# Cross-attention block with a four-layer FFN: both first transposes of the probabilities moved behind the third step of the second FFN layer

## The reference

```python
x = x + xattn(layernorm(x), ctx)     # 8 heads of 32, causal mask, softmax over 77 keys
x = x + ffn(layernorm(x))
# ffn: h = silu(x w1 * s1) * (x w2 * s2)       256 -> 1024
#      h = gelu(h h1 * s)                      1024 -> 1024
#      h = gelu(h h2 * s)                      1024 -> 1024
#      out = h w3 * s3                         1024 -> 256
```

## Time and profile before

| | us |
|---|---|
| median of 3 runs | 1674.82 (1674.29 to 1677.77) |
| the profiled execution, its own time | 1673.74 |
| its span in the profile | 1671.6 |
| PE busy | 1617.4 (97%) |
| PE weight loads | 1311.9 (78%) |
| DVE busy | 806.5 (48%) |
| ACT busy | 783.5 (47%) |
| POOL busy | 139.4 (8%) |

### The profile page before, as it was taken

One profiled execution on the slowest core, in us unless ns is written; L12 is line 12 of the kernel. 1 busy time (PEld: TensorE's weight loads), 2 busy tenths in 40 slices (PEclk: granted clock), 3 DMA queues, 4 the chain that ended last, 5 costly groups with the idle time before them and its releaser, 6 DMA issues.

```text
span 1671.6 us, 22062 instructions
## 1 busy us (share of the span) xinstructions
PE 1617.4 (97%) x9006; PEld 1311.9 (78%) x9006; DVE 806.5 (48%) x1255; ACT 783.5 (47%) x1126; POOL 139.4 (8%) x136
## 2 busy tenths in 40 slices
PE   5599999999999999999999999999999999999998
PEld 4378788787887878878787887878878787887887
DVE  5563634637255463634637255463544636345331
ACT  4463644636345363543636345363543635345342
POOL 1101102010010200102010010200102010010000
PEclk7699999999999999999999999999999999999999
DMA  8100000010000100000010000100001010000000
GB/s 328 43 1 26 29 25 29 0 42 13 25 29 0 54 0 25 29 25 29 0 42 13 25 29 0 52 2 25 29 11 43 0 40 14 25 30 1 1 13 13
DMA packets 17638, 48.40 MB, mean 29 GB/s; under 512 B 5584, under 2 KB 7760, under 8 KB 16208
## 3 DMA queue, kind: packets, MB, share of 16 engines
q1 hardware_dynamic: 17616, 48.09, 8.0%
HBM read 39.63 MB, written 8.45 MB: 29 GB/s over the span
## 4 chain that ended last, share of the span: by engine, by line
PE 88%; DVE 6%; ACT 3%; issue 2%; DMA 0%; POOL 0%; POOLq 0%; SPq 0%; ACTq 0%
PE ffn_banks L348 69%; PE att_banks L484 4%; PE att_banks L503 3%; PE att_banks L456 3%; PE att_banks L472 2%; PE att_banks L493 2%; PE att_banks L447 2%; DVE probs L702 1%; DVE total L698 1%; ACT L579 1%; ACT probs L579 1%; DVE a_f L662 1%; PE att_banks L442 1%; PE att_banks L511 1%; DVE a_lo L667 1%
## 5 line engine op out<-in xcount | busy, mean ns | idle before, releaser
L348 PE MATMUL ffn_banks<-a_hi,h_sb 128*128 128x512 f32 x1024 | 408.9, 399 | 0.0
L348 PE MATMUL ffn_banks<-b_hi,h_sb 128*128 128x512 f32 x1024 | 401.3, 392 | 0.0
L348 PE MATMUL ffn_banks<-a_lo,h_sb 128*128 128x512 f32 x1024 | 400.2, 391 | 0.0
L348 PE MATMUL ffn_banks<-b_lo,h_sb 128*128 128x512 f32 x1024 | 398.6, 389 | 0.0
L554 ACT ACTIVATE a_f<-ffn_banks,vec 128x512 f32<-128x512 f32 x128 | 88.2, 689 | 354.2 <-PE ffn_banks L348 354.2
L673 DVE TENSOR_TENSOR a_lo<-a_f,a_hi 128x512 fp32r<-128x512 f32 x128 | 88.6, 692 | 317.8 <-ACT a_hi L555 317.8
L348 PEld LDWEIGHTS ffn_banks<-a_hi,h_sb 128*128 128x128 f32 x1024 | 192.3, 188 | 48.9 <-issue 6.2
L348 PEld LDWEIGHTS ffn_banks<-b_lo,h_sb 128*128 128x128 f32 x1024 | 192.3, 188 | 39.8
L348 PEld LDWEIGHTS ffn_banks<-b_hi,h_sb 128*128 128x128 f32 x1024 | 192.3, 188 | 39.8
L348 PEld LDWEIGHTS ffn_banks<-a_lo,h_sb 128*128 128x128 f32 x1024 | 192.5, 188 | 38.5
L348 PE MATMUL ffn_banks<-ln_hi,w_sb 128*128 128x512 f32 x512 | 213.8, 418 | 6.2 <-issue 6.2
(11 more groups left out here) (89 smaller groups left out, 1952.5 us busy)
## 6 DMA issues: line engine op xcount, KB each, us to landing
x_in<-in_x SPq DMA_DIRECT2D x16, 512.0 KB, 3.5
h_bits<-in_h SPq DMA_DIRECT2D x8, 1024.0 KB, 20.8
out<-out_sb SPq DMA_DIRECT2D x16, 512.0 KB, 2.6
ln_t<-in_x_t SPq DMA_DIRECT2D x15, 512.0 KB, 4.3
ln_rows<-ln_rows_dram SPq DMA_DIRECT2D x15, 512.0 KB, 3.8
w_bits<-in_w SPq DMA_DIRECT2D x3, 1024.0 KB, 10.1
ctx_sb<-in_ctx_t SPq DMA_DIRECT2D x16, 154.0 KB, 3.6
w_att_sb<-in_w_att SPq DMA_DIRECT2D x1, 512.0 KB, 5.8
```

The lines of the kernel that those rows point to most:

```text
L348: mm = nc.tensor.matmul(psum, left, right, start=(k == 0 and part == 0), stop=(k == rows - 1 and part == 1))
```

## The change

The list ORDER is changed in one line. The two first transposes stand together behind ("L2", 2), and ("SOFT", 1) stands behind both of them. FIRST is unchanged.

```diff
-    ("PT", 0), ("SOFT", 1), ("L2", 2), ("PT", 1), ("L2", 3), ("PV", 0), ("PT", 2), ("L2", 4), ("PT", 3),
+    ("L2", 2), ("PT", 0), ("PT", 1), ("SOFT", 1), ("L2", 3), ("PV", 0), ("PT", 2), ("L2", 4), ("PT", 3),
```

## The result

The changed kernel took 1730.64 us (median of 4 runs, 1727.26 to 1731.76) beside 1674.55 for the kernel before: a ratio of 1.0329 with a 95% interval of 1.0308 to 1.0350. Run again beside other kernels on another occasion it took 1731.69 us. The time lies in the forecast range, 1.2 us under the lower end of the rival in which the clock falls as well (1731.8 to 1740.8), and not near the likeliest case (1706.3).

A forecast was written before the change was run, and what follows sets the result against it. PE's order and waits bound the kernel, PT0 coming as late as half 0's scaling. PT2 2.10 us later in 15 passes (31.5 us), on 1673.74 plus 1.08 to the median, gave 1706.3 us; range 1702 to 1742.

The forecast's parts named there:

- the rival in which the clock falls as well: PE's clock also falls to half around PT2, in many or all woven passes: 1731.8 to 1740.8 us in all 15; chance 0.39.
- the likeliest case: Only waits move: PT2 2.10 us later in each of 15 passes, giving 1706.3 us, or 1703 to 1713 with spread.
- the order of the steps that the prediction lists: Chain before PT2: exponentials, Gelu table load, L2.2's two Gelus, DVE's subtraction, two copies, SOFT1; PT2 at 622.56 against 620.46.
- the lower bound: DVE's distance from one PSUM copy to the next instruction without a wait: at least 0.60 us, at most 0.78.
- PE's 1.05 us: Gain per pass for PE alone: 0.87 us of standing still before PT0 and one break of the stream less.
- the point from which the rival decides: At PT2, rival that SOFT1 is in time (1659.0 us, chance 0.04): SOFT1 must end by 620.34 to be no slower.
- the case with the clock up: Waits moved in the woven passes, PE's clock staying up or fallen in a few passes only; chance 0.53.
- the two slow cases: In the woven passes, waits moved with the clock up, 0.53, or the clock falling in many or all, 0.39.
- a stretch of 1.7 us: On PE from 609.35 to 611.07, with one group of transposes, it cost nothing; cited against the clock falling.
- The price of a fall: Time PE loses when its clock drops to half: at least 1.7 us, 2.3 for a longer fall.
- the later wait: PE standing still 2.2 us before PT2 for SOFT1, said to cover PV0's lateness of about 1.0 us.

The follow-up runs named there:

- e5: Changed kernel with 8 idle products on PE behind PV0, before PT2, in each of the 15 woven passes; 1704.87 us, ratio 1.0187 to the kernel before.
- e4: Changed kernel with PE's order kept, but ACT and DVE doing their part of L2.2 behind SOFT1; 1660.86 us, ratio 0.9910 to the kernel before.
- e6: Changed kernel with half 1's exponentials replaced by Gelu in the woven passes, so no table load before L2.2's Gelus; 1700.61 us, ratio 1.0158.
- e8: Changed kernel with 4 idle products on PE in the gap before PT2; 1707.87 us, ratio 1.0189 to the kernel before.
- e7: Changed kernel unaltered, run again beside other kernels; 1731.69 us, ratio 1.0342 to the kernel before.
- e2: Changed kernel with PT0 alone moved back in front of L2.2; 1707.03 us, ratio 1.0183 to the kernel before.
- e3: Changed kernel with SOFT1 alone moved back ahead of L2.2 and the two copies; 1688.83 us, ratio 1.0072 to the kernel before.
- e1: Changed kernel with 18 idle products on PE behind PV0, before PT2, in each of the 15 woven passes; 1735.49 us, ratio 1.0358.

## Why the prediction came out as it did

**Right: the direction and the mechanism.** PT2 now waits for SOFT1, SOFT1 for L2.2's subtraction and the copies, in the order of the steps that the prediction lists. Its terms, held against the changed kernel's second woven pass: from the table load's start to the scaling's end 221.75 + 1.45 - 215.60 = 7.60 us, forecast 622.44 - 614.81 = 7.63. The distance between the two copies, the only one the trace of before did not show, is 0.60 (in the third pass two copies begin at 321.49 and the sum behind them at 322.69), the lower bound. From the scaling's end to PT2 it is 223.25 - 223.20 = 0.05, forecast 0.12. PT2 is 1.98 us late, forecast 2.10, and these two small terms make up most of the difference; the waits cost 29.8 us (e5), forecast 31.5. PE's idling before PV0 and PT2 was forecast at 1.0 and 2.2 and is 0.94 and 1.95.

**Right: the gain that is lost.** e4 shows that PE's 1.05 us were there to be had, 1.00 as measured, and that the point from which the rival decides is where the prediction put it: SOFT1 has to be done before PE wants PT2.

**Right: the table load.** 1.28 us as in the earlier trace rows; e6 takes 1.31 off the period. The 1.38 us of drain besides it, which "ScalarE: Activation LUTs" of the Trainium skill states under "What ACT_TABLE_LOAD costs", are nowhere on this path: the Gelu starts 1.30 us behind the load's start (215.60 to 216.90).

**Wrong: which case is the likeliest.** The step that failed is the weighing of "The clock falls as well". I gave it 0.39 and the case with the clock up 0.53; it fell in 13 and 15 of 15 passes. (The chances of the two slow cases add up to 0.92, where the text has 0.93 for slower.) The first pass's fall after a stretch of 4.90 us with 2.26 us of work was the right row. I set against it that PV0 and PT2 are larger products than those of that stretch, and that a stretch of 1.7 us had cost nothing. Neither saved this kernel: the clock fell behind 5.0 us with 2.12 us of work, in two idle pieces of which none is longer than 2 us, and e5 and e8 show that it was this idling that took the clock, for with 0.9 and 1.8 us of it there is no fall.

The price of a fall was a little too high: I gave 1.7 us as the least, and the single falls cost 1.3 to 1.6, in part because several begin while PE still waits for PT2 (for the PT2 at 430.18 the clock is at half from 429.6 on). That the rival's lower end, 1731.8 for 1.7 us in each pass, agrees with the measured 1730.64 is partly luck: falls of double length in two passes (three in e7) bring the mean to 1.71 over fewer falls.

The Trainium skill's page "TensorE: Matmul & The Clock Gate" ("HAM oscillation — how this bites in real kernels") warns of gaps in which PE idles. Read as speaking of one wholly idle piece, it would have spared this kernel, whose longest piece is 1.95 us; the trace disagrees, with falls in 13 and 15 of 15 passes.

**Not foreseen:** what PT0's move does, which I had booked as harmless beside the later wait. It adds the idle piece before PV0, and with it most of the falls: of the loss of 56 us e2 leaves 31.

What stays open is what decides, beside the idling, in which passes the clock falls. e6 and e2 differ in it by 10 to 2 though e6 idles less, and in e3 the clock fell in 5 passes with 1.5 us of waiting. The period of the pass differs between them too, and with it the moments at which the passes come; no run varied that alone, and none varied the kind of the products between the idle pieces. So a part of e2's gain may be owed to its moments and not to its shorter idling.

## What to carry to other kernels

When one list orders all engines, a step that is moved for PE drags its parts on ACT and DVE along, and these can put a long chain (here a table load, two Gelus and a subtraction) ahead of something that PE will soon need. Follow the moved step on every engine, and where only one engine gains, move it for that engine alone: e4 turned a loss of 3.3% into a gain of 0.9%. When a change makes PE idle between dense products, price the clock as well as the wait, even where each piece is short: here it nearly doubled the loss. The passes with a fall went from none at 1.8 us of idling to 13 and 15 of 15 at 2.9 us, with the period unchanged, and e6 had 10 at 1.6 us with another period. A few products of no use in the gap, short enough not to delay the next step, took the falls away (e5); too many cost as much as they won (e1).

## What was not expected of the hardware

- PE's clock fell after short idle pieces (0.94 and 1.95 us) with 1 us of products between them, and in most passes though not in all.
- A fall of the usual length cost 1.3 to 1.6 us and one of double length 2.9, 1.71 as a mean; eight small products of no use in each pass (1.98 us on PE, in a gap) were worth 26.8 us over the run.
- A float32 product of 128x128 by 128x128 is two instructions of 0.12 us (36 for 18 in e1), while the transpose of a 128x77 block through the identity is one, of about 0.10.
